# Attention and a mixture of experts on one core: transposes and projections share four PSUM banks

## What is computed

```python
xn = _layernorm(x)
q, k, v = proj(Wq, bq), proj(Wk, bk), proj(Wv, bv)          # 16 heads of 32
scores = einsum('bhqd,bhkd->bhqk', q, k) / sqrt(32)
scores = where(causal, -inf, scores) + alibi
probs = softmax(scores)
attn = einsum('bhqk,bhkd->bhqd', probs, v) -> (b, s, 512) @ Wo.T + bo
probs_e = softmax(xn @ gate_w.T);  topw, sel = top_k(probs_e, 2)
act = silu(g) * u                                            # g, u: xn through w1 of the expert
ffn = sum over the two experts of weight * (act @ w2.T)
return x + attn + ffn
```

## Time and profile before

| | us |
|---|---|
| median of 3 runs | 1607.26 (1606.22 to 1608.5) |
| profiled execution, its own time | 1608.96 |
| its span, first to last instruction | 1607.2 |
| TensorE busy | 1469.5 (91%) |
| DVE busy | 1042.5 (65%) |
| ACT busy | 888.6 (55%) |
| GpSimd busy | 568.5 (35%) |
| mean granted TensorE clock, share of full | 0.976 |

### The profile page before, as it was taken

One profiled execution on the slowest core, in us unless ns is written; L12 is line 12 of the kernel. 1 busy time (PEld: TensorE's weight loads), 2 busy tenths in 40 slices (PEclk: granted clock), 3 DMA queues, 4 the chain that ended last, 5 costly groups with the idle time before them and its releaser, 6 DMA issues.

```text
span 1607.2 us, 35535 instructions
## 1 busy us (share of the span) xinstructions
PE 1469.5 (91%) x12763; PEld 892.2 (56%) x12763; DVE 1042.5 (65%) x2500; ACT 888.6 (55%) x2020; POOL 568.5 (35%) x595
## 2 busy tenths in 40 slices
PE   4899989998898999999899898999789999999995
PEld 2565545654565555556555466555356656656662
DVE  7887786666878767777788877777243333333331
ACT  5677686665768767676776465777122222222221
POOL 5111232121123213113222233221217777777675
PEclk9999999998999999999999899999899999999998
DMA  7355231442433255443214233145777889788893
GB/s 258 103 140 133 86 107 50 121 123 79 131 93 110 66 146 149 124 131 92 80 59 123 84 97 91 39 146 140 274 189 123 134 126 146 131 138 132 127 143 46
DMA packets 171350, 193.28 MB, mean 120 GB/s; under 512 B 87536, under 2 KB 121072, under 8 KB 171056
## 3 DMA queue, kind: packets, MB, share of 16 engines
q1 hardware_dynamic: 143760, 151.67, 34.6%
q0 software_dynamic: 26128, 37.24, 14.2%
q10 hardware_dynamic: 1296, 2.11, 0.3%
HBM read 93.45 MB, written 53.74 MB: 92 GB/s over the span
## 4 chain that ended last, share of the span: by engine, by line
PE 66%; DVE 11%; issue 6%; DMA 5%; SPq 4%; ACT 3%; POOL 2%; POOLq 0%; DVEq 0%; ACTq 0%
PE S L1224 15%; PE T L1147 11%; PE O L1163 7%; PE S L1104 5%; PE S L1136 5%; PE M L1104 4%; PE M L1255 4%; PE O L1255 4%; DVE arena L1528 4%; SPq L979 4%; PE M L1186 2%; DMA out<-arena 2%; PE S L1121 2%; DVE arena L1544 2%; PE S L1186 1%
## 5 line engine op out<-in xcount | busy, mean ns | idle before, releaser
L1528 DVE CUSTOM_DVE_ANT_0 arena<-S,cF,nsl 128x1024 f32<-128x1024 f32 (+7 forms) x512 | 413.1, 811 | 70.3 <-PE S L1136 48.5
L1725 ACT ACTIVATE arena<-arena,mneg 128x1024 f32<-128x1024 f32 (+7 forms) x512 | 395.6, 773 | 57.2 <-DVE mneg L1528 56.6
L1147 PE MATMUL T<-cF,arena 128*128 128x128 f32 x2304 | 366.3, 280 | 66.1 <-ACT arena L1742 37.3
L1742 ACT ACTIVATE arena<-T 128x512 f32<-128x512 f32 (+3 forms) x532 | 241.6, 467 | 250.7 <-PE T L1147 247.9
L1147 PEld LDWEIGHTS T<-cF,arena 128*128 128x128 f32 x2304 | 267.7, 142 | 169.3 <-issue 49.0
L1224 PE MATMUL S<-arena 128*128 x1704 | 269.8, 315 | 10.0 <-issue 9.9
L1881 POOL DMA_INDIRECT out<-arena x142 | 222.1, 1564 | 107.6 <-ACT arena L1788 57.9
L1224 PEld LDWEIGHTS S<-arena 128*128 128x128 f16 x1704 | 167.7, 98 | 109.1 <-issue 11.3
L1544 DVE COPY arena<-T 128x512 f32<-128x512 f32 (+3 forms) x300 | 153.2, 514 | 108.3 <-PE T L1147 106.5
L1163 PE MATMUL O<-arena 128*32 128x128 f32 (+1 forms) x3328 | 213.6, 333 | 6.8 <-DVE arena L1564 5.7
L1136 PE MATMUL S<-arena 96*128 96x512 f16 (+3 forms) x768 | 212.8, 331 | 3.1 <-DVE mneg L1528 1.8
(11 more groups left out here) (190 smaller groups left out, 1821.6 us busy)
## 6 DMA issues: line engine op xcount, KB each, us to landing
arena<-arena SPq DMA_DIRECT2D x192, 128.0 KB, 2.4
arena<-in_w1T SPq DMA_DIRECT2D x64, 352.0 KB, 3.5
arena<-in_x SPq DMA_DIRECT2D x64, 256.0 KB, 3.5
w_d<-arena SPq DMA_DIRECT2D x32, 352.0 KB, 2.9
arena<-w_d SPq DMA_DIRECT2D x16, 704.0 KB, 6.7
arena<-in_w2T SPq DMA_DIRECT2D x32, 256.0 KB, 2.9
out<-arena SPq DMA_DIRECT2D x32, 256.0 KB, 3.0
xn_d<-arena SPq DMA_DIRECT2D x24, 256.0 KB, 2.2
```

Source lines behind the costliest of these rows:

```text
L1147: tp = pe.transpose(z[:, (c - c0) * P:(c - c0 + 1) * P], ring[u % 4][:, c * P:(c + 1) * P], idf)
L1528: dve.tensor_tensor_reduce(ring[r][:, 0:w], SBK[o.bank["score", u]][:, 0:w], rel[:, S - w:S], nsl[:, hh:hh + 1], 3.0e38, ALU.add, ALU.min, ...
L1725: act.activation(ring[r][:, 0:w], ring[r][:, 0:w], ACT.Exp, bias=mneg[:, m:m + 1], scale=-1.0, accum_out=rs[:, k, c:c + 1]).then_inc(sems[ ...
L1742: act.activation(PT[k][:, h, to_:to_ + gap * (c1 - c0 - 1) + 1:gap, :], TB[o.bank["tr", u, i]][:, 0:n].rearrange("p (c n) -> p c n", n=P), ...
```

## The change

Transposes of probabilities, x-transposes, projections, gates, ranks and lists take their banks from one pool of four: T0, T1, M and the second bank of S1. A bank is `borrow`ed until the step that empties it is added to the list (`give`), and `borrow` takes, among those that no one holds, the one that was given back longest ago in the list. The user then waits for the step that emptied this bank. The two "T" banks of the experts' stage become a pool "X" of their own with the same two banks; its first users wait for the last users of the shared pool.

```diff
-        self.size = {"S": 2, "T": 2, "O": 1, "M": 2, "Y": 2}
+        self.size = {"S": 2, "O": 1, "X": 2, "Y": 2}
...
+        self.since, self.owner = dict.fromkeys(range(4), 0), {}
...
+    def borrow(self, *key):
+
+        i = min((i for i in range(4) if i not in self.owner), key=lambda i: self.since[i])
+        self.owner[i] = key
+        self.bank[key] = i
+        self.emptied[key] = self.tenant.get(("B", i), [])
+
+    def give(self, key, *steps):
+        i = self.bank[key]
+        del self.owner[i]
+        self.since[i] = len(self.steps)
+        self.tenant[("B", i)] = list(steps)
...
     def take_m(*key):
         if len(later) > 1:
             flush()
-        o.take("M", *key)
+        o.borrow(*key)
...
         for i, (c0, c1, at, gap) in enumerate(turn_parts(u)):
             if (i > 1) != late:
                 continue
-            o.take("T", "tr", u, i)
+            o.borrow("tr", u, i)
             add("tr", u, i)
             yield
             en = lighter((c1 - c0) * P)
             add("pt", u, i, en, sem="pt" + en)
             o.count["pt", u, i] = o.count["pt", u, i, en]
-            o.leave("T", ("tr", u, i), ("pt", u, i))
+            o.give(("tr", u, i), ("pt", u, i))
...
-    s1, m1 = o.tenant["S", 1], o.tenant["M", 1]
+    s1, m1 = o.tenant["S", 1], o.tenant["B", 3]
     o.tenant["S", 1] = s1 + m1
-    o.tenant["Y", 0], o.tenant["Y", 1] = o.tenant["O", 0], o.tenant["M", 0]
-    o.turn["T"] = 0
+    o.tenant["Y", 0], o.tenant["Y", 1] = o.tenant["O", 0], o.tenant["B", 2]
+    o.tenant["X", 0], o.tenant["X", 1] = o.tenant["B", 0], o.tenant["B", 1]
...
-    MBK = [ps("M", [P, 512], F32), GU[1][:, 512:1024]]
-    YB = [OB, MBK[0]]
+    MB = ps("M", [P, 512], F32)
+    PB = [*TB, MB, GU[1][:, 512:1024]]
+    YB = [OB, MB]
...
-                z = TB[o.bank[step]]
+                z = PB[o.bank[step]]
                 for c in range(c0, c1):
                     tp = pe.transpose(z[:, (c - c0) * P:(c - c0 + 1) * P], ring[u % 4][:, c * P:(c + 1) * P], idf)
                 tp.then_inc(sems["tr"], 1)
```

More of the change, by code:

```diff
@@ L188, in ln_turn @@
         key = "xtp", b, half, i
[L189 to L193, removed]
+        take_m(*key)
         add(*key)
@@ L199, in rest @@
             o.count["xt", b, half, i] = o.count["xt", b, half, i, en]
-            o.leave(bank, key, ("xt", b, half, i))
+            o.give(key, ("xt", b, half, i))
         later.append(rest)
@@ L214, in rest @@
             add("lg", b)
-            o.leave("M", ("gate", b), ("lg", b))
+            o.give(("gate", b), ("lg", b))
         later.append(rest)
@@ L230, in rest @@
             add("qk32", b, g, qk, half)
-            o.leave("M", key, ("qk32", b, g, qk, half))
+            o.give(key, ("qk32", b, g, qk, half))
             load["act"] += 0.7
@@ L257, in rest @@
             add("vsb", b, g, half)
-            o.leave("M", key, ("vsb", b, g, half))
+            o.give(key, ("vsb", b, g, half))
         later.append(rest)
@@ L335, in rest @@
             add("y", b, i)
-            o.leave("M", key, ("y", b, i))
+            o.give(key, ("y", b, i))
         later.append(rest)
@@ L410, in routing @@
         add("route", 12)
-        o.leave("M", ("rank",), ("route", 12))
+        o.give(("rank",), ("route", 12))
         yield
@@ L431, in rest @@
                 add("listsum", c)
-                o.leave("M", ("lists", c), ("listsum", c))
+                o.give(("lists", c), ("listsum", c))
             later.append(rest)
@@ L530, in widest @@
         flush()
-        o.take("M", "gmax", what, part)
+        o.borrow("gmax", what, part)
         add("gmax", what, part)
@@ L534, in widest @@
         add("gtop", what, part)
-        o.leave("M", ("gmax", what, part), ("gtop", what, part))
+        o.give(("gmax", what, part), ("gtop", what, part))
         yield
@@ L1055, in tensor @@
                     on.wait_ge(*at(*s))
-                tz = (MBK if key[0] else TB)[o.bank[step]][:, :].bitcast(F16)
+                tz = PB[o.bank[step]][:, :].bitcast(F16)
                 k = half_place(*key)
@@ L1062, in tensor @@
                 b, part = key
-                z = MBK[o.bank["gate", b]]
+                z = PB[o.bank["gate", b]]
                 if part == 0:
@@ L1079, in tensor @@
                 what, part = key
-                z = MBK[o.bank["gmax", what, part]]
+                z = PB[o.bank["gmax", what, part]]
                 c, n = (LW, 3) if what == "w" else (LWO, 1)
@@ L1093, in tensor @@
                 b, g, qk, half, third = key
-                z = MBK[o.bank["qk", b, g, qk, half]]
+                z = PB[o.bank["qk", b, g, qk, half]]
                 if third == 0:
@@ L1109, in tensor @@
                 b, g, half, i = key
-                z = MBK[o.bank["v", b, g, half]]
+                z = PB[o.bank["v", b, g, half]]
                 if i == 0:
@@ L1415, in vector @@
                 tt = half * 4 + i
[L1416 removed]
+                tz = PB[o.bank["xtp", b, half, i]][:, :].bitcast(F16)
                 on.wait_ge(*at("xtp", b, half, i))
@@ L1681, in scalar @@
                 tt = half * 4 + i
-                tz = (MBK if b else TB)[o.bank["xtp", b, half, i]][:, :].bitcast(F16)
+                tz = PB[o.bank["xtp", b, half, i]][:, :].bitcast(F16)
                 on.wait_ge(*at("xtp", b, half, i))
```

27 lines of the change are left out of this document (13 added, 14 removed).

## The result

| | us |
|---|---|
| median after, 9 runs | 1593.32 (1592.27 to 1602.52) |
| median before, the 9 runs beside them | 1607.26 (1600.77 to 1614.79) |
| ratio after/before, 95% interval | 0.9926 (0.9910 to 0.9941) |
| profiled execution of after, its own time | 1593.44 |
| its span | 1591.6 |

The change makes the kernel 14 us faster; 30 us had been forecast. In a later comparison the same kernel took 1595.96 us against 1608.58, a ratio of 0.9909 (0.9882 to 0.9935). The time lies inside the stated range (1552 to 1600 us); the direction and the kind of gain held (waits at the transposes), and less than half of the gain came. Lines of the code are 11 higher than before in what follows: the transposes are L1158, their copies L1753 (ACT) and L1555 (DVE), the scores L1147 and the row minimum L1539, the values (`pv`) L1174 and `a32`, which frees their bank O, L1575.

The account below looks back on a forecast made before the run. TensorE was taken to bound the kernel, with 86 us idle in attention to gain from. Terms 8 + 23 - 3 + 2 = 30 us off 1608.96 gave 1579, stated as 1577 us for the median, range 1552 to 1600.

Parts of the forecast that it names:

- Kind 1: Seven long waits at the transposes, 17.0 us in all, where the new rule names the same copy; nothing of them goes.
- Kind 2: Nine other waits over 1.3 us at the transposes, 18.1 us in all; followed one by one, 8 us gained.
- Kind 3: The remaining short waits at the transposes, 29.5 us in all; together 23 us to be gained.
- some fourteen are kept nearly whole: Waits at a unit's third transpose group, whose copy stands behind an ACT exponential; 10 us, gained nearly whole.
- Term 4: In stretches where DVE is full, an earlier TensorE finds the same DVE; half of some 6 us, 3 us, given back.
- Term 5: In attention, clock falls go where waits go wholly: 2 us gained, at most some 9 us.
- Term 6: Projections, gates and x-transposes share banks with T's copies; banks were emptied in time, nearest by 0.4 us, so no cost.
- rival that the clock swings more: TensorE's clock falls double with four banks in turn; 22 us of the 30 lost, 1599 us; chance 0.02.
- rival that ended slower: First matmuls of some 125 projections wait behind ACT copies, 58 us against 30 gained, 1635 us; chance 0.06.
- ACT and DVE are the limit after all: In attention TensorE runs ahead into the next wait each time; 0 to 12 us gained, 1595 to 1607 us; chance 0.14.
- the change does not do what it says: Copies stay two groups behind for most transposes and nothing moves; no separate chance, counted within the 0.14 rival's no-change part.

## Why the prediction was wrong in size

**What bounds the kernel** was read rightly: the gain lies in TensorE's idle time in attention, and the experts moved as a block. The terms are compared with the two profiled executions, one instruction of TensorE with the same one.

**Kind 1, nothing kept: right, and slightly worse than that.** The five long ones, 4.91, 2.80, 2.68, 2.26 and 2.26 us (14.9), are 4.86, 3.59, 2.75, 3.04 and 3.04 us (17.3). The two of about 1 us are 1.08 and 1.80, so 20.2 us stand in place of 17.0. TensorE arrives earlier at the same late copy. The reason given (two other users hold a bank each) fits the run with a fifth bank, where three of these no longer wait for that copy; but other waits took most of their time.

**Kind 2, 8 us of 18.1 kept: about 3.** At the transposes 9.0 us are left of the nine. Another 3.7 us stand at scores and values right behind them (0.90 and 0.39 behind the 2.19 us, 0.44 and 0.48 behind the 2.50, 1.45 behind the 1.60), and 2.6 us at projections and lists (0.38, 0.65 and 1.59): 18.1 - 9.0 - 3.7 - 2.6 = 2.8 us. The 1.74 us, of which all was to be kept, went at the transposes, but the list matmul that follows within 4 us waits 1.59 us for GpSimd, for which it had not waited before. Of the 3.32 us, 1.5 were to be left; 2.93 are.

**Kind 3, 23 us of 29.5 kept: about 12. This is the mis-sized term.** At the transposes the short waits did go as said: 4.6 us are left, for the 6.5 forecast. But of the 17.1 us that came at the values and the scores, 3.7 us belong to kind 2, as above, and the other 13.4 are counted here as kind 3 come back: 29.5 - 4.6 - 13.4 = 11.5 us. The step that failed is "some fourteen are kept nearly whole" and its like: the working had followed each short wait to the next transposes and to the score, one at a time. What the traces show is that several kept waits meet the next buffer together, as above, where a score waits 1.10 us in place of the 0.48 and 0.18 us at the transposes ahead of it. The forecast of 5 to 10 us at the scores held (9.2 more); the 7.9 us at bank O had no term at all. A term for bank O alone would not have been the cure: with O in the pool, three quarters of its waits went on to the scores.

**Term 4, given back where DVE is full, -3 us: the place was right, the size and the reason were not.** In the stretches with layer norm (units 64 to 112, 192 to 240 and 320 to 384), the waits at the transposes fell from 26.7 to 16.0 us, and those at the values, scores and projections rose from 2.7 to 12.2: 9.4 of the 10.7 us came back there. By the starts of their scores these stretches gained 1.8 us in all. In the other units up to 496 the waits at the transposes fell by 19.7 us, and those at the values and scores rose by 8.2. But cutting the statistics from DVE changed nothing of this: between the two kernels with the cut, 9.7 us went and 9.1 came in the same stretches. So DVE's statistics are not the reason, and moving copies off DVE gave nothing either. What else of the layer norm, on DVE or ACT, stands ahead of L1575 and L1539 there is open, and no run gave the scores a third bank.

**Term 5, the clock, +2 us: not there, and rather of the other sign.** In the profiled pair the mean granted clock is 0.975 for 0.976, and in attention 0.97 for 0.98. Over all runs whose clock is on record the median is 0.973 for the changed kernel (15 runs) and 0.977 for the kernel before (46 runs). Among those 46, a clock lower by 0.001 goes with 1.3 us more, so 0.004 would be some 5 us; this is an estimate, and no run tells whether the clock or the waits come first. The rival that the clock swings more with four banks in turn forecast twice the falls; what is missing of the full clock rose from 0.023 to 0.027, by a sixth. The Trainium skill, page "TensorE: Matmul & The Clock Gate", section "A second HAM failure mode: psum-queue depth-cycling", describes such swings in another kernel that goes round PSUM banks. Here the step from two banks to four agrees with it in sign alone, and five are no lower than four: about 0.974, and 0.977 with the hold spread.

**Term 6, projections behind copies, 0 us:** nearly right. `qk` waits 1.1 us more, the lists 2.5 us more, the output projection and the x-transposes no more than before. The rival that ended slower needed 30 us here.

**The rivals.** "ACT and DVE are the limit after all" gave 1595 to 1607, and the time is just below its end. It is partly right: over the whole of attention no engine is full, but TensorE does run ahead into the next wait, behind DVE's steps (L1539, L1575). That the change does not do what it says is refuted by the traces, in which the transposes' waits fall from 66.1 to 33.8 us.

Added up: 32.3 us less at the transposes (about 40 were forecast), 9.2 more at the scores (5 to 10), 7.9 more at bank O (0), 3.6 more at the lists and `qk` (0), and 3.8 us less of busy time. Put into the prediction's sum, kind 3 at 11.5 in place of 23, kind 2 at 2.8 in place of 8, kind 1 at -3.2, and nothing for term 4 (what was given back is in the kinds now) and the clock give 11.1; the lists and `qk` take the 1.0 us that kind 2 has not yet counted, and 3.8 of busy time and 1.5 of waits at the transposes that the 64.6 us had not counted come to it: 15.4 us, as the traces have it.

The distance between the two orders of banks depends on where steps fall. It is 14 us in the order as given and with the shorter statistics, but 21 us with the hold spread, 25 with the values sooner and 28 with both holds spread. Two banks lose by each shift, or gain less, than four do.

## What to carry to other kernels

When a pool of buffers is widened, follow the engine that is set free through every resource of its round, and with all the waits removed together: the time that comes back stands at the next buffers, and it was nearly two thirds of the relief here. Widening that next one too may only send the wait one buffer further, as bank O's went to the scores. Share banks among users by the age of their last release only together with enough banks, since three were worse than two and two, and the lowest free number cost a quarter of the time. The longest wait came from an engine held by another engine, neither four banks nor five helped there, and putting the held step some turns later was worth nearly as much as the whole change.

## What had not been expected

One hold of DVE behind a GpSimd reduction (7.38 us, of which TensorE stands 4.86) cost 9 to 10 us of attention, twice its visible wait. The granted clock from 360 to 380 us was 0.74 with the hold, and 1.00 in the run with the hold spread. And with the lowest free bank the time rose by 391 us, while the two largest rows of waits make only 216.5 of it. Of the 387 us by which its profiled span is longer, 243 are idle time of TensorE, spread over many rows, and 144 are longer busy time, at a mean granted clock of 0.932 in place of 0.976.
